# Self-attention over 2048 keys: the 32 steps as one written-out sequence instead of a loop of 8 steps on the engines

## The chip, the core and the metric

The kernel runs on one core of one Trainium2 chip. The metric is the device time of one execution in microseconds (us). The core has five engines that run their own instruction streams and meet only at semaphores: TensorE (PE; its weight loads are listed as PEld), VectorE (DVE), ScalarE (ACT), GpSimd (POOL) and SyncE (SP), which here issues the DMAs.

## The reference, cut to what matters

Two transformer blocks on x of shape 2 x 2048 x 512, with 16 heads of 32 channels: a cross-attention block, then a block of self-attention, cross-attention and MLP. The part around the change is the self-attention of the second block:

```python
def mha(q, k, v):                       # q, k, v: 2 x 2048 x 512, d = 32, H = 16
    scores = jnp.einsum('bqhd,bkhd->bhqk', qh, kh) / jnp.sqrt(d)
    attn = jax.nn.softmax(scores, axis=-1)
    out = jnp.einsum('bhqk,bkhd->bqhd', attn, vh)
    return out.reshape(B, Nq, C)
...
h = mha(q, k, v) @ self_o_w + self_o_b
x = x + h * gate_msa
```

## The kernel before, in words

`build` runs these stages one after the other: `conditioning`, `cross_pass` p1, `dense_pass` p2 (which makes q, k and v), `attention` a2 (from about 905 to 2807 us of the profiled span), `cross_pass` p3 and `mlp`. Only `attention` is touched.

`attention` works on 32 steps (`STEPS`). A step is one of 2 batches, one of 4 groups of 4 heads, and one of 4 chunks of 512 queries. Within a step PE makes the scores twice. In one form, queries on partitions (`score_unit`, tile a_sm, line L1797, 64 matmuls a step), DVE takes the maximum of each row (`peak_of_unit`, L1957), and from these `minus_peaks` (L1964 to L1973) makes the values that are subtracted. In the other form, keys on partitions (`score_tile`, tile a_st, L1819, 64 matmuls a step), ACT takes the exponential (`exponentials`, tile a_e, L1911). PE multiplies the exponentials with v (`weigh`, L1832) and adds them up (`add_up`, L1848) into tile a_acc; POOL adds part of them up beforehand (a_esum, L2029). Once a step ACT copies the two sums out (`fetch_sums`, tile a_sums, L1925), at the beginning of the step that follows; PE waits for this copy before it may write a_acc again. So the starts of the 32 a_sums copies cut the trace into steps: the copy of step n stands near the beginning of step n + 1. The peaks of a step are made two steps and one step ahead of its exponentials.

The order of the work on each engine is the order in which its function issues it; nothing reorders it. Each engine function ends in `run(engine, step, first, late)`. It writes out step 0 (for SP, steps 0 and 1), then opens a hardware loop, `engine.Fori(0, STEPS // BODY - 1)`, with `BODY` = 8 steps in its body, which is run 3 times, and then writes out what is left. On PE, steps 1 to 24 are in the loop and steps 25 to 31 are written out. In the loop the number of the iteration is in a register, so that every semaphore value that is waited for has to be worked out by register instructions (REGISTER_ALU in the listings below, ALU_OP and FUSED_REGOPS in the trace); in the written-out steps it is a constant. Each engine has its own loop and its own branch back (L1703), and the branches are not synchronized with each other.

`bank_of_unit` gives the PSUM bank of a score unit by `(j % BODY + u) % RING`. As 8 x 64 units aren't a multiple of the 3 banks, the sequence of banks breaks off at every eighth step, and `score_unit` then waits for one more read (`j % BODY == 0 and u < 2`).

Of the kernel before, what the change touches and what calls it, by code (L numbers as in the profile page):

```python
# [21 lines left out]
CHUNKS = T // W  # L22
# [1569 lines left out]
def attention(nc, d, name, q_in, k_in, v_in, o_out, keys, preload):  # L1592
# [21 lines left out]
    QR = 4  # L1614
# [2 lines left out]
    POOLED = [t for t in range(NKT - 2) if t % 3 != 2] if NKT > 2 else []  # L1617
    ADDS = max(len(POOLED) - 1, 0)
    STEPS = B * GROUPS * CHUNKS
    BODY = 2 * CHUNKS  # L1620
    TURN_KT = max(NKT - 3, 0)
    TURN = GH * (TURN_KT + 1)
    HEAD = 14 if NKT > 1 else U
# [5 lines left out]
    with nc.cleanup_on_exit(), ExitStack() as ctx:  # L1629
# [38 lines left out]
        def exists(i, j):  # L1668

            return not isinstance(i, int) or 0 <= BODY * i + j < STEPS  # L1670

# [4 lines left out]
        def number(i, j, p):  # L1676


            return (BODY * i + j) * TILES + p + (p < TURN or exists(i, j + 1))

        def turned(i, j):

            return number(i, j - 1, TURN) if j else 0
# [6 lines left out]
        def bank_of_unit(j, u):  # L1690

            return (j % BODY + u) % RING

# [4 lines left out]

        def run(engine, step, first, late):

            for j in range(first):
                step(0, j)
            with engine.Fori(0, STEPS // BODY - 1) as i:  # L1703
                for j in range(first, BODY + first):
                    step(i, j)
            for j in range(first, BODY + late):
                step(STEPS // BODY - 1, j)

        @block.sync
        def _(sp):  # L1710
            for dst, src in ((ident[:], d["ident"]), (mask[:], d["mask"])):
                sp.dma_start(dst, src).then_inc(small_in, DMA)
            for s in o_stored:
                sp.sem_inc(s, DMA)

            def load_q(i, j):

                for row, part in enumerate((0, 0, 1)):
                    src = q_in[part].rearrange("b (g h r) t -> (b g) r h t", g=GROUPS, h=GH)
                    sp.dma_start(q[row * DH:(row + 1) * DH, j % QR].bitcast(F32),  # L1720
                                 src[2 * i + j // CHUNKS, :, :, j % CHUNKS * W:(j % CHUNKS + 1) * W]
                                 ).then_inc(q_loaded[j % QR], DMA)

            def load_k(i, g):

                for row, part in enumerate((0, 1, 0)):
                    src = k_in[part].rearrange("b (g h r) t -> (b g) r h t", g=GROUPS, h=GH)
                    sp.dma_start(k[row * DH:(row + 1) * DH, g % 2, :, 0:keys].bitcast(F32),
                                 src[2 * i + g]).then_inc(k_loaded[g % 2], DMA)

            def load_v(i, g):
                sp.dma_start(v[0:KR, g % 2], v_in[(i + g // 2) // 2, :, bass.ds(((i + g // 2) % 2 * 2 + g % 2) * P, P)].rearrange("(t p) c -> p t c", p=KR)
                             ).then_inc(v_loaded[g % 2], DMA)

            def spread_rows(i, j):

                sp.wait_ge(score_read, turned(i, j) + 3)
                sp.dma_start(q[3 * DH:P, j % QR].bitcast(F32), rows[3 * DH:P, j % 2].unsqueeze(1).to_broadcast([DH, GH, W])
                             ).then_inc(rows_ready[j % QR], DMA)

            def store_o(i, j):
                sp.wait_ge(scaled, BODY * i + j + 3)


                sp.sem_inc(passed, 1)
                dst = o_out.rearrange("b (g p) t -> (b g) p t", p=P)
                sp.dma_start(dst[2 * i + j // CHUNKS, :, j % CHUNKS * W:(j % CHUNKS + 1) * W],
                             o[:, j % 2]).then_inc(o_stored[j % 2], DMA)

            def step(i, j):  # L1750
                if exists(i, j - 1) and exists(i, j + QR - 1):

                    sp.wait_ge(score_done, (BODY * i + j) * TILES + 1)
                    sp.sem_inc(passed, 1)
                if exists(i, j + QR - 1):
                    load_q(i, j + QR - 1)
                if j % CHUNKS == 0 and exists(i, j + CHUNKS):
                    load_k(i, j // CHUNKS + 1)
                    if exists(i, j - 1):

                        sp.wait_ge(tile_used, (BODY * i + j) * NKT + ER)
                        sp.sem_inc(passed, 1)
                    load_v(i, j // CHUNKS + 1)
                if exists(i, j - LATE - 1):
                    store_o(i, j - LATE - 1)
                if exists(i, j + 1):
                    spread_rows(i, j + 1)

                if isinstance(i, int) and i > 0 and 0 <= j - (BODY - QR) < len(preload):
                    sp.dma_start(*preload[j - (BODY - QR)]).then_inc(preloaded, DMA)  # L1770

            load_q(0, 0)
            load_k(0, 0)
            load_v(0, 0)
            for j in range(1, QR - 1):
                load_q(0, j)
            spread_rows(0, 0)
            run(sp, step, LATE + 1, LATE + 1)
            for s in o_stored:
                sp.wait_ge(s, DMA * (STEPS // 2 + 1))  # L1780
            sp.wait_ge(preloaded, DMA * len(preload))

        @block.tensor
        def _(pe):
# [103 lines left out]
            for u in range(HEAD):  # L1888
                score_unit(0, 1, u)
            run(pe, step, LATE, 1)  # L1890

        @block.scalar
        def _(act):
# [50 lines left out]
            act.activation(k[3 * DH:P, 0], mask[3 * DH:P].unsqueeze(2).to_broadcast([DH, GH, KC * KE]), ACT.Copy).then_inc(act_set_up, 1)  # L1944
            take_rows(0, 0)
            run(act, step, LATE, 1)

        @block.vector
# [286 lines left out]
def build(nc, d, out):  # L2235
# [17 lines left out]
    with nc.sbuf_tensor("mod", [P, MODS, B], F32) as mod:  # L2253
        def vector_of(tile):
            return lambda b, t: mod[:, tile + t, b:b + 1]

        with ExitStack() as ctx:
            raw_qkv, load_qkv = raw_weights(ctx, "raw_qkv", *[w("L1_xcond_qkv_w", c) for c in range(3)])
            with ExitStack() as inner:
                raw, load = raw_weights(inner, "raw_p1", d["L0_xcond_Wq"], d["L0_xcond_Wp"])  # L2260
                conditioning(nc, d, mod, gates, kv, load)
                cross_pass(nc, d, "p1", d["x"], x1, None, kv[0][0], kv[0][1], q, (1e-5, vector_of(0), vector_of(4)),
                           (1e-6, vector_of(20), vector_of(16)), d["L0_xcond_bq"], d["L0_xcond_bp"], u, raw, load_qkv)
            dense_pass(nc, d, "p2", u, [(vec("L1_xcond_qkv_b", 0), q), (vec("L1_xcond_qkv_b", 1), k)], (vec("L1_xcond_qkv_b", 2), v), raw_qkv)
        with ExitStack() as ctx:
            raw, load = raw_weights(ctx, "raw_p3", d["L1_xcond_self_o_w"], d["L1_xcond_q_w"], d["L1_xcond_cross_o_w"])
            attention(nc, d, "a2", q, k, v, o, T, load)
            cross_pass(nc, d, "p3", x1, x3, (o, d["L1_xcond_self_o_w"], d["L1_xcond_self_o_b"], gates[0]), kv[1][0], kv[1][1], q,
                       (1e-6, lambda b, t: mod[:, 40 + t, 0:1], lambda b, t: mod[:, 40 + t, 1:2]), (1e-6, vector_of(32), vector_of(28)),
                       d["L1_xcond_q_b"], d["L1_xcond_cross_o_b"], u, raw, [])  # L2270
        mlp(nc, d, u, x3, gates[1], out)
# [19 lines left out]
```

## Time and profile before

| what | value |
|---|---|
| device time, median of 3 runs | 4163.22 us (4161.48 to 4164.41) |
| device time of the profiled execution | 4159.49 us |
| span of the profiled execution, first to last instruction | 4157.7 us |
| mean granted TensorE clock | 0.938 of 2.4 GHz |
| PE busy | 3771.6 us, 91% |
| DVE / POOL / ACT busy | 2333.9 / 2080.2 / 1867.3 us, 56 / 50 / 45% |

The span runs from the first instruction to the last; 1.8 us of the profiled execution lie around it. A busy share is an average over stages that have different limits, so the rows below are cut to the attention stage. Of a timeline row the first number is the start, the second the duration, and in brackets stands how long the engine sat idle before it and what ended that. A matmul's duration overlaps the next one's; the pace of PE is read from the starts.

### The profile page before, as it was taken

Reading aid. Unit: us, or ns where it says so; the run is one execution under the profiler, and the core shown is the slowest. Engines: PE = TensorE matmul, PEld = TensorE weight load, DVE = VectorE, ACT = ScalarE, POOL = GpSimd, SP = SyncE. Lnnn points to the kernel's source line nnn. Section 1 sums busy time; section 2 is a strip of 40 time slices with the busy share of each in tenths; the row PEclk is TensorE's granted clock in tenths of the full one; section 3 lists DMA queues with packets and bytes.
Section 4 is the critical chain, followed back from the end, with each engine's and each line's share of the span. In section 5 each row is a group of like instructions: output and inputs, shape, how many; then the busy total and the mean of one; then the engine's idle time right before and its main releaser. Section 6 shows DMA issues by size and latency. Waiting matters only on the chain. (4 is left out here: it accounts for less than half of the span.)

```text
span 4157.7 us, 58861 instructions
## 1 busy us (share of the span) xinstructions
PE 3771.6 (91%) x19596; PEld 2442.6 (59%) x19596; DVE 2333.9 (56%) x4020; ACT 1867.3 (45%) x3431; POOL 2080.2 (50%) x923
## 2 busy tenths in 40 slices
PE   4799969979999999999999999985999959999998
PEld 2577748854444444444444444433777737888887
DVE  2466642247777767776777777733676625222222
ACT  1465631115666656665666666663565521111111
POOL 0356630005778767776777777783676634000000
PEclk8788879978999999999999999997999869999999
DMA  7566657752130211203130211105567651211110
GB/s 230 133 158 173 168 154 220 227 137 62 26 67 16 64 27 38 46 23 67 26 67 15 65 26 26 31 18 134 135 165 173 164 166 56 81 40 40 40 40 30
DMA packets 213560, 371.98 MB, mean 89 GB/s; under 512 B 36103, under 2 KB 52999, under 8 KB 209703
## 3 DMA queue, kind: packets, MB, share of 16 engines
q1 hardware_dynamic: 213287, 368.49, 32.7%
q8 instruction: 153, 2.51, 0.3%
q14 instruction: 120, 0.98, 0.1%
HBM read 215.54 MB, written 144.51 MB: 87 GB/s over the span
## 5 line engine op out<-in xcount | busy, mean ns | idle before, releaser
L1957 DVE TENSOR_REDUCE a_peak<-a_sm 128x1 f32<-128x512 f32 x2048 | 1275.0, 682 | 470.5 <-PE a_sm L1797 464.5
L1911 ACT ACTIVATE a_e<-a_st 128x512 f32<-128x512 f32 x2048 | 1075.1, 600 | 718.2 <-PE a_st L1819 714.7
L2029 POOL TENSOR_TENSOR a_esum<-a_esum,a_e 128x2048 f32<-128x2048 f32 x256 | 1172.1, 4578 | 126.5 <-ACT a_e L1911 114.1
L1819 PE MATMUL a_st<-a_q,a_k 128*128 128x512 f32 x2048 | 870.2, 428 | 17.9 <-issue 12.9
L1797 PE MATMUL a_sm<-a_k,a_q 96*128 96x512 f32 x2048 | 831.8, 413 | 49.7 <-DMA a_k<-s_k 28.1
L1819 PEld LDWEIGHTS a_st<-a_q,a_k 128*128 128x128 f32 x2048 | 386.4, 189 | 536.7 <-ACT a_e L1911 269.9
L1832 PE MATMUL a_acc<-a_e,a_v 128*32 128x512 f32 x4096 | 547.2, 606 | 17.6 <-ACT a_sums L1925 16.7
L1797 PEld LDWEIGHTS a_sm<-a_k,a_q 96*128 96x128 f32 x2048 | 397.8, 194 | 148.8 <-DVE a_peak L1957 57.6
L2152 PE MATMUL mlp_ph<-mlp_us,mlp_w_hi 128*128 128x512 f32 x1024 | 336.3, 391 | 31.9 <-DVE mlp_raw_lo L2201 31.9
L2029 POOL TENSOR_TENSOR a_esum<-a_e 128x2048 f32<-128x2048 f32 x32 | 146.8, 4587 | 427.6 <-ACT a_e L1911 427.6
L2194 ACT ACTIVATE mlp_gelu<-mlp_ph,mlp_b 128x512 f32<-128x512 f32 x128 | 88.1, 688 | 595.4 <-PE mlp_ph L2152 595.4
L2209 DVE CAST mlp_gs<-mlp_gelu 128x512 fp32r<-128x512 f32 x128 | 91.4, 714 | 458.3 <-ACT mlp_gelu L2194 458.3
L2167 PE MATMUL mlp_py<-mlp_w_hi,mlp_gs 128*128 128x512 f32 x1024 | 317.7, 391 | 17.1 <-DVE mlp_gs L2211 17.1
L2232 POOL TENSOR_TENSOR mlp_x<-mlp_x,mlp_brow 128x2048 f32<-128x2048 f32 x8 | 37.0, 4626 | 569.5 <-DMA mlp_x<-s_x 569.3
L1409 POOL TENSOR_TENSOR p_e<-p_e,p_inv 128x308 f32<-128x308 f32 x256 | 173.4, 709 | 168.6 <-DVE p_inv L1093 168.6
L2152 PEld LDWEIGHTS mlp_ph<-mlp_us,mlp_w_hi 128*128 128x128 f32 x1024 | 193.2, 189 | 72.6 <-issue 32.3
L2167 PEld LDWEIGHTS mlp_py<-mlp_w_hi,mlp_gs 128*128 128x128 f32 x1024 | 192.0, 188 | 61.6 <-issue 16.5
L587 PE MATMUL p_sm<-p_ks,p_qs 96*128 96x78 f32 x1024 | 171.9, 310 | 47.7 <-DMA p_qs<-s_q 28.3
L587 PEld LDWEIGHTS p_sm<-p_ks,p_qs 96*128 96x128 f32 x1024 | 157.2, 222 | 80.9 <-issue 28.9
L1848 PE MATMUL a_acc<-a_e,a_ones 128*32 128x512 f32 x1536 | 201.4, 596 | 1.7 <-POOL a_esum L2029 1.7
L2167 PE MATMUL mlp_py<-mlp_raw_lo,mlp_gs 128*128 128x512 f32 x512 | 200.0, 391 | 0.0
L2152 PE MATMUL mlp_ph<-mlp_us,mlp_raw_lo 128*128 128x512 f32 x512 | 199.9, 390 | 0.0
(151 smaller groups left out, 5169.7 us busy)
## 6 DMA issues: line engine op xcount, KB each, us to landing
p_qs<-s_q SPq DMA_DIRECT2D x192, 256.0 KB, 5.7
s_q<-p_qo SPq DMA_DIRECT2D x64, 512.0 KB, 7.4
a_q<-s_q SPq DMA_DIRECT2D x96, 256.0 KB, 5.2
a_k<-s_k SPq DMA_DIRECT2D x24, 1024.0 KB, 15.5
s_x<-p_x SPq DMA_DIRECT2D x16, 1024.0 KB, 4.4
s_u<-p_ut_hi SPq DMA_DIRECT2D x64, 256.0 KB, 5.8
s_u<-p_ut_lo SPq DMA_DIRECT2D x64, 256.0 KB, 6.4
p_us<-s_u SPq DMA_DIRECT2D x16, 1024.0 KB, 7.8
```

Source lines behind the costliest of these rows:

```text
L587: mm = pe.matmul(sm[:, unit % 2, h * KE:(h + 1) * KE], qs[0:3 * DH, g % 2, h, qt * P:(qt + 1) * P], ks[0:3 * DH, b, g * GH + h], start=Tru ...
L1409: pool.tensor_tensor(e[:, number % 2, qt, :, 0:S], e[:, number % 2, qt, :, 0:S], inv[:, number % 2, qt].unsqueeze(2).to_broadcast([P, GH, ...
L1797: mm = pe.matmul(sm[:, bank_of_unit(j, u), x * KE:(x + 1) * KE], q[0:3 * DH, j % QR, h, qt * P:(qt + 1) * P], k[0:3 * DH, g % 2, h, kc * K ...
L1819: pe.matmul(st[0:KR, place(kt, h) % RING], k[:, g % 2, h, kt * P:kt * P + KR], q[:, j % QR, h], start=True, stop=True).then_inc(score_done, 1)
L1832: mm = pe.matmul(acc[rows, 0], v[0:KR, g % 2, kt, rows], e[0:KR, (j * NKT + kt) % ER, h], start=(kt == 0), stop=(kt == NKT - 1), tile_posi ...
L1848: mm = pe.matmul(acc[h * DH:(h + 1) * DH, 1], ones[0:KR], operand[:, h], start=(kt == first), stop=(kt == NKT - 1 and x == len(operands) - ...
L1911: act.activation(e[0:KR, (j * NKT + kt) % ER, h], st[0:KR, place(kt, h) % RING], ACT.Exp, scale=SCALE).then_inc(score_read, 1)
L1957: dve.tensor_reduce(dst, src, AX.X, ALU.max).then_inc(unit_read, 1)
L2029: pool.tensor_tensor(esum[:], e[:, slot(0)] if x == 1 else esum[:], e[:, slot(x)], ALU.add).then_inc(e_added, 1)
L2152: mm = pe.matmul(ph[:, m % 4], w1[pw][:, t, m * P:(m + 1) * P], us[:, b, pm, t], start=(t == 0 and s == 0), stop=(t == KT - 1 and s == 2))
L2167: mm = pe.matmul(py[:, tt], gs[:, m % 2, pw, tt * P:(tt + 1) * P], w2[pm][:, m], start=(m == 0 and s == 0), stop=(m == HT - 1 and s == 2))
L2209: dve.tensor_copy(gs[:, m % 2, 0], gelu[:, m % 2]).then_inc(g_hi, 1)
```

## The change

`BODY` becomes 32, and `run` writes all steps out, on all five engines. The loop, its branches and the register instructions are gone, and every wait is against a constant. The condition under which SP preloads the weights of the next stage is adapted and holds at the same steps as before (28 to 30). With `j % BODY` now `j`, the banks go round without a break, and the additional read is asked for at step 0 alone, where it was already given.

```diff
-    BODY = 2 * CHUNKS
+    BODY = STEPS
...
         def run(engine, step, first, late):
 
-            for j in range(first):
+            for j in range(STEPS + late):
                 step(0, j)
-            with engine.Fori(0, STEPS // BODY - 1) as i:
-                for j in range(first, BODY + first):
-                    step(i, j)
-            for j in range(first, BODY + late):
-                step(STEPS // BODY - 1, j)
...
-                if isinstance(i, int) and i > 0 and 0 <= j - (BODY - QR) < len(preload):
+                if 0 <= j - (BODY - QR) < len(preload):
```

The lines below the edit move up by five: L1797 becomes L1792, L1819 becomes L1814, L1925 becomes L1920.

PE at the end of the loop's body, late in step 8 (and 16 and 24), before the change: L1688 and L1795 are the register instructions for a wait, L1703 is the loop's end.

```order
 L1848 MATMUL a_acc<-a_e,a_ones 32x512 x4
 L1819 MATMUL a_st<-a_q,a_k 128x512
 L1795 REGISTER_ALU
 L1797 MATMUL a_sm<-a_k,a_q 128x512
 L1688 REGISTER_ALU
 L1819 MATMUL a_st<-a_q,a_k 128x512
 L1795 REGISTER_ALU
 L1797 MATMUL a_sm<-a_k,a_q 128x512
 L1703 REGISTER_ALU
 L1703 COMPARE_AND_BRANCH
 L1819 MATMUL a_st<-a_q,a_k 128x512
```

The last of these rows is where the loop is left after step 24. The same place of a step after the change:

```order
 L1843 MATMUL a_acc<-a_e,a_ones 32x512 x4
 L1814 MATMUL a_st<-a_q,a_k 128x512
 L1792 MATMUL a_sm<-a_k,a_q 128x512
 L1814 MATMUL a_st<-a_q,a_k 128x512
 L1792 MATMUL a_sm<-a_k,a_q 128x512
 L1814 MATMUL a_st<-a_q,a_k 128x512
```

The matmuls stand in the same order; the register instructions and the branch between them are gone.

DVE where a step's peaks become the values to subtract, before the change (the last peak of a step, then L1962 to L1973, then the first peaks of the step after the next):

```order
 L1954 REGISTER_ALU
 L1957 TENSOR_REDUCE a_peak<-a_sm 128x1
 L1962 ISA
 L1964 TENSOR_REDUCE a_top<-a_peak 128x16
 L1966 TENSOR_SCALAR a_neg_hi<-a_top 128x16
 L1969 ISA
 L1972 COPY a_neg<-a_neg_hi 128x4x4
 L1973 SCALAR_TENSOR_TENSOR a_neg<-a_top,a_neg_hi 128x4x4
 L1953 REGISTER_ALU
 L1954 REGISTER_ALU
 L1957 TENSOR_REDUCE a_peak<-a_sm 128x1 x2
```

And after it:

```order
 L1952 TENSOR_REDUCE a_peak<-a_sm 128x1 x17
 L1959 TENSOR_REDUCE a_top<-a_peak 128x16
 L1961 TENSOR_SCALAR a_neg_hi<-a_top 128x16
 L1967 COPY a_neg<-a_neg_hi 128x4x4
 L1968 SCALAR_TENSOR_TENSOR a_neg<-a_top,a_neg_hi 128x4x4
 L1952 TENSOR_REDUCE a_peak<-a_sm 128x1 x21
```

Here too only the register instructions between the operations are gone.

## Rows read from the trace of the kernel before

**Rows 1.** The page: busy time of the engines in the whole span.
```profile
PE 3771.6 (91%) x19596; PEld 2442.6 (59%) x19596; DVE 2333.9 (56%) x4020; ACT 1867.3 (45%) x3431; POOL 2080.2 (50%) x923
```

**Rows 2.** All instructions on the tile a_sums: durations min/median/max, first and last start.
```profile
L1925 ACT ACTIVATE a_sums<-a_acc x32: 1024/1027/1032, 1015.3 to 2803.0; 128x1024 f32<-128x1024 f32 x32
```

**Rows 3.** Busy time in windows cut at starts of a_sums copies; columns in the first line.
```profile
core 0: us, PE busy (x) PEld busy (x) DVE busy (x) ACT busy (x) POOL busy (x), PEclk, DMA share, GB/s
1015.30:1417.19 401.89, 392.85 (x2213) 192.99 (x2212) 303.02 (x498) 247.14 (x470) 296.93 (x70) 1.00 0.15 34
1417.19:1483.81 66.62, 58.80 (x318) 28.46 (x316) 43.49 (x72) 35.40 (x69) 42.41 (x10) 0.92 0.40 90
1483.81:1885.72 401.91, 392.88 (x2213) 193.00 (x2212) 302.99 (x498) 247.02 (x470) 296.92 (x70) 1.00 0.15 34
1885.72:1951.88 66.16, 58.34 (x318) 28.36 (x316) 43.49 (x72) 35.41 (x69) 42.41 (x10) 0.95 0.41 91
1951.88:2411.34 459.46, 449.01 (x2529) 220.65 (x2528) 346.37 (x569) 282.30 (x537) 339.43 (x80) 1.00 0.19 42
2411.34:2697.50 286.16, 280.38 (x1581) 138.00 (x1580) 216.99 (x356) 178.31 (x336) 212.23 (x50) 1.00 0.10 27
```

**Rows 4.** PE's timeline over the end of the loop's first run.
```profile
1468.93 0.40 PE L1797 MATMUL a_sm<-a_k,a_q 96*128 96x512 f32 x1
1475.77 0.80 PE L1819 MATMUL a_st<-a_q,a_k 128*128 128x512 f32 x1 [6.44 <-issue]
...
1482.29 0.50 PE L1819 MATMUL a_st<-a_q,a_k 128*128 128x512 f32 x1
```

**Rows 5.** PE's timeline over the end of the loop's second run.
```profile
1944.28 0.80 PE L1819 MATMUL a_st<-a_q,a_k 128*128 128x512 f32 x1 [6.44 <-issue]
...
1950.36 0.50 PE L1819 MATMUL a_st<-a_q,a_k 128*128 128x512 f32 x1
```

**Rows 6.** PE's timeline where the loop is left, after its third run.
```profile
2405.53 0.40 PE L1797 MATMUL a_sm<-a_k,a_q 96*128 96x512 f32 x1
2406.00 0.47 PE L1819 MATMUL a_st<-a_q,a_k 128*128 128x512 f32 x1
...
2409.83 0.50 PE L1819 MATMUL a_st<-a_q,a_k 128*128 128x512 f32 x1
```

**Rows 7.** PE's timeline where the loop is entered.
```profile
1009.54 0.40 PE L1797 MATMUL a_sm<-a_k,a_q 96*128 96x512 f32 x1
1009.91 0.50 PE L1819 MATMUL a_st<-a_q,a_k 128*128 128x512 f32 x1
```

**Rows 8.** PE's branch at the end of the attention's loop: ns min/median/max, first and last.
```profile
L1703 PEldq COMPARE_BRANCH  x3: 82/3568/3758, 1467.0 to 2403.6; - x3
```

**Rows 9.** The same for PE's branch at the end of the MLP's loop.
```profile
L2172 PEldq COMPARE_BRANCH  x4: 76/222/240, 3612.6 to 4143.7; - x4
```

**Rows 10.** DMA queues from 1464 to 1484 us, at the first branch back.
```profile
q8 instruction: 3, 0.05, 1.0%
```

**Rows 11.** DMA queues from 2420 to 2650 us, in written-out steps.
```profile
q8 instruction: 10, 0.16, 0.3%
```

**Rows 12.** DMA queues from 3620 to 4150 us, in the MLP's loop: all lines.
```profile
q1 hardware_dynamic: 11616, 23.07, 12.0%
```

**Rows 13.** PE's timeline at the change of steps, in the loop (step 13).
```profile
1754.33 0.39 PE L1819 MATMUL a_st<-a_q,a_k 128*128 128x512 f32 x1
1755.48 0.50 PE L1797 MATMUL a_sm<-a_k,a_q 96*128 96x512 f32 x1 [0.76 <-DVE a_peak L1957]
```

**Rows 14.** The same place in a written-out step (step 26).
```profile
2509.30 0.39 PE L1819 MATMUL a_st<-a_q,a_k 128*128 128x512 f32 x1
2510.30 0.50 PE L1797 MATMUL a_sm<-a_k,a_q 96*128 96x512 f32 x1 [0.62 <-DVE a_peak L1957]
```

**Rows 15.** PE's groups over the five written-out steps, 2411.34 to 2697.50 us.
```profile
L1797 PE MATMUL a_sm<-a_k,a_q 96*128 96x512 f32 x321 | 127.5, 397 | 3.2 <-DVE a_peak L1957 3.2
L1832 PE MATMUL a_acc<-a_e,a_v 128*32 128x512 f32 x640 | 85.2, 605 | 2.2 <-ACT a_sums L1925 2.2
```

## The prediction

> **What bounds the kernel now.** I read the page first. PE is busy 91% of the span, every other engine at most 59% [rows 1]. That points to PE, but a share over the whole span can't price an edit of one stage, so I cut the attention stage at the starts of the a_sums copies, of which there is one a step [rows 2], into the windows of [rows 3]. Their columns show which engine sets the pace: in the 401.89 us of steps 1 to 7 PE is busy 392.85 us (98%), DVE 303.02, POOL 296.93 and ACT 247.14, and the granted clock is 1.00. So PE is the bound inside attention, and only what holds up PE counts. The other four engines get rid of their loops too; they have 14 us or more to spare in each step of 57.4 us.
>
> The same windows hold the answer to most of the question, because the kernel before runs the same step in both forms. Steps 1 to 24 go through the loop, 25 to 31 are written out. [Rows 3]: 7 looped steps take 401.89 us (57.41 each), the next window is one step and takes 66.62, then 401.91 for 7, 66.16 for one, 459.46 for 8 (57.43 each), and then 286.16 us for five written-out steps, which is 57.23 each. The two long windows are steps 8 and 16, where the first two runs of the loop end. Step 24 also ends a run of the loop, but there the branch isn't taken, and its window has no such excess.
>
> **The change part by part.**
>
> *The two branches back.* The 22 ordinary looped steps take (401.89 + 401.91 + 459.46) / 22 = 57.42 us. Steps 8 and 16 exceed this by 9.20 and 8.74, together 17.94 us. The timeline says what they consist of. Between the last matmul before the branch (start 1468.93) and the first behind it (1475.77) lie 6.84 us, with PE idle for 6.44 and "issue" as the reason: no semaphore was late, the engine had no instruction [rows 4]. In ordinary code the two starts would be some 0.23 us apart, as 1009.54 lies 0.37 from its successor even with the loop's entry between them [rows 7]; so 6.6 us are lost. Then PE runs slowly: the durations are 0.80 where 0.50 is usual, the window's clock is 0.92, and the piece of work up to the next a_st after the additions takes 6.52 us (1475.77 to 1482.29) [rows 4]. The same piece where the loop is left takes 3.83 (2406.00 to 2409.83) [rows 6], so 2.7 us go to PE standing at its lower clock level of 1.2 GHz after the pause. 6.6 + 2.7 = 9.3, against 9.20 measured. The second time it is 6.6 + (6.08 - 3.83) = 8.85, against 8.74 [rows 5]. Both parts go when the pause goes.
>
> Is the pause really the branch's? PE's branch record is 3568 and 3758 ns long on two occasions and 82 ns on the third, which falls through [rows 8]. Queue q8, which carries instructions, made 3 transfers in the 20 us around the first branch [rows 10], and 10 in 230 us of written-out steps, one per 23 us [rows 11]. So behind a taken branch PE's instructions are fetched anew. In the MLP's loop, whose body is much shorter, q8 isn't in the list of queues at all [rows 12], and the branch that is taken lasts 222 to 240 ns [rows 9]. What is dear is thus not a branch but a branch to code that has to be fetched. Without the loop, nothing jumps, and the fetch runs ahead as it does in the written-out steps.
>
> A rule of the Trainium skill speaks against this sum. "Advanced Engine Details and Errata", section Control Flow Timing, puts a compare-and-branch at about 108 ns. By that the loop's three branches on PE would be worth 0.3 us, and the pauses would belong to something that stays. The trace agrees for the branch that falls through (82 ns) and not for the two that are taken into unfetched code (3568 and 3758 ns) [rows 8]; the rows decide, and the rule's case is the second rival below.
>
> *The register instructions.* A written-out step takes 57.23 us, a looped one 57.42 [rows 3], 0.19 less. One place where it comes from is the change of steps, where PE waits for DVE's peak reductions: 0.76 us idle in the loop [rows 13], 0.62 written out [rows 14], because DVE works out two wait values between its small operations and its next peak. Over 24 steps this makes 24 x 0.19 = 4.5 us. All of it is on PE's path, since PE is the bound. Over the five written-out steps PE has just 3.2 us of idle time before that place and 2.2 us before a_acc, where ACT copies the sums [rows 15]; no other wait is behind these, so no new one takes their place: the written-out steps show what is late next, and it is the same two waits, shorter.
>
> *Entry and exit of the loop.* At the entry two starts are 0.37 us apart instead of 0.23 [rows 7], 0.14 us, before the first window. The exit (0.47 instead of 0.23 us) [rows 6] lies in the last looped window and is counted.
>
> *The banks and the additional read.* These cost nothing before: the first units of step 8, at which the banks break off, are scored in steps 6 and 7, which lie in the 401.89 us of seven even steps [rows 3]. I take them at nothing. *The preload and all the DMAs* are issued by SP in the same order, at the same steps. *The loads of k and v at every fourth step* are issued in steps 4 to 24, which are all looped; the five written-out windows hold none. The window of 8 steps has two of them and 57.433 us a step, those of 7 steps have one and 57.413 [rows 3]. So a step with loads takes up to 0.18 us more (0.02 divided by 2/8 - 1/7), from register work for its additional waits or from the loads themselves. In the second case 6 x 0.18 = 1.1 us of the gain would be missing. I take the first, since the bulk of the difference between the forms is of that kind, and keep the other for the range.
>
> *Sum.* 17.9 + 4.5 + 0.14 = 22.6 us (the short way: 1396.04 us for steps 1 to 24 minus 24 x 57.232 = 22.5, plus the entry). Against the profiled execution's own 4159.49 us this gives 4136.9. That execution was 3.7 us faster than the median of the runs shown, 4163.22; from the median I get 4140.6 us, and this is what I predict.
>
> *Bounds.* At the low end the steps keep their looped pace and only the branches go: 17.9, that is 4145.3. The high end: the largest excess that looped windows show, 57.43, against 57.23 for every step, and half a microsecond for entry and exit, is 17.9 + 4.8 + 0.5 = 23.2, that is 4140.0. To these comes what the runs differ by, 2.9 us from fastest to slowest. The stages behind attention shift by 22 us as a whole; their work is unchanged, and I put them at nothing, plus or minus the runs' own difference. The range is 4137 to 4147.
>
> **The rivals.**
>
> *Only the branches pay.* The step's pace could stay at 57.42, if the written-out steps at the end are faster for another reason, such as the missing loads of k and v. For it: the five steps are the last ones and hold fewer transfers (27 GB/s against 34) [rows 3]. Against it: a shorter idle time at a place that has to do with DVE and not with a load [rows 13, 14]. Time 4145.3.
>
> *The pause isn't the branch's.* The pauses stand at the end of steps 8 and 16, just behind the loads for a new group of heads and two steps behind the break of the banks; if something of this kind made PE wait, the pause would stay, and only the register instructions and the loop's ends would be gained: 4.5 + 0.14 = 4.6, time 4158.6. For it: only two events, at equal distance. Against it: PE's idle time is "issue" [rows 4, 5], the end of step 24 is the same place behind such loads and such a break, and has no pause [rows 6], and the branch's own record is long [rows 8].
>
> *Slower: fetching the long code isn't hidden.* The place is PE's instruction stream in steps 1 to 24, the price one exposed fetch per 23 us. There would be 24 x 57.2 / 23 = 60 of them. One takes about 0.3% of 16 x 230 us over 10, 1.1 us [rows 11]; exposed in full they cost 66 us, and the kernel would take 4163.2 + 66 - 22.6 = 4206.6. It decides from 22.6 / 60 = 0.38 us a fetch on. Against it: in the five written-out steps 12 fetches passed and PE's only idle times are the two waits for DVE and ACT [rows 15]. For it: just that what was seen of written-out attention code ran with few other transfers.
>
> *The change doesn't do what it says* is out: the listing has no branch between the steps.
>
> **How the numbers follow.** The forecast 0.73, only the branches 0.13, the pause stays 0.05, exposed fetches 0.05, something unnamed 0.04. What can be told from no change in a measurement of this kernel is about 0.2%, 8.3 us: below 4154.9 it is faster. The forecast, the first rival and half of the unnamed are faster: 0.88. The second rival and a little of the unnamed are within 0.2%: 0.06. The rest, 0.06, is slower. The range 4137 to 4147 holds the forecast and the first rival, 0.86 less a little for their tails.
>
> **What would show each step right or wrong.** In the profile of the changed kernel, with windows cut at the a_sums copies: steps 1 to 24 in about 1373.6 us, every step at 57.2 to 57.3, steps 8 and 16 like the others; no COMPARE_BRANCH in attention; the granted clock at 1.00 from step 1 to the end of attention without a dip at a step; q8 with one transfer per 23 us all the way; PE idle 0.62 us at the change of steps in all steps. The forecast is wrong if a pause with the reason "issue" stands anywhere in attention, if steps that load k and v are slower than the others by more than 0.2 us, or if the stages after attention change by more than 3 us.

## The result, and the profile after

| | before | after |
|---|---|---|
| median of 7 runs | 4163.22 us | 4144.30 us |
| lowest to highest | 4154.85 to 4166.21 | 4137.23 to 4152.43 |
| ratio of the runs | | 0.9957, 95% interval 0.9944 to 0.9969 |
| profiled execution, its span | 4159.49, 4157.7 | 4145.81, 4144.0 |

By the medians the kernel is faster by 18.9 us; the interval of the ratio gives 12.9 to 23.3. Predicted were 22.6 us and 4140.6, with a range of 4137 to 4147. The ratios in this text compare fast runs with fast runs; one execution of the kernel with PE alone written out, of 11039.88 us, is left out of them.

The page of the profile after has the same 19596 matmuls; the program as executed has 51860 records instead of 58861. Register and branch instructions are 7769 fewer, and 768 more instructions on semaphores stand in the written-out code.

```profile
span 4144.0 us, 51860 instructions
PE 3766.3 (91%) x19596; PEld 2441.2 (59%) x19596; DVE 2335.7 (56%) x4020; ACT 1877.2 (45%) x3431; POOL 2080.8 (50%) x923
```

The windows below are cut at the starts of the a_sums copies, as in [rows 3], with the same columns: steps 1 to 7, step 8, steps 9 to 15, step 16, steps 17 to 24, steps 25 to 29.

```profile
1011.13:1412.07 400.94, 392.72 (x2214) 193.22 (x2212) 303.94 (x498) 249.88 (x471) 297.10 (x70) 1.00 0.15 34
1412.07:1469.37 57.30, 56.12 (x318) 27.60 (x316) 43.43 (x72) 35.67 (x69) 42.45 (x10) 1.00 0.45 100
1469.37:1870.47 401.10, 392.80 (x2214) 193.23 (x2212) 303.98 (x498) 249.79 (x471) 297.15 (x70) 1.00 0.15 34
1870.47:1927.77 57.30, 56.12 (x318) 27.60 (x316) 43.43 (x72) 35.67 (x69) 42.45 (x10) 1.00 0.46 100
1927.77:2386.00 458.23, 448.87 (x2529) 220.84 (x2528) 347.34 (x569) 285.58 (x538) 339.57 (x80) 1.00 0.19 42
2386.00:2672.50 286.50, 280.57 (x1581) 138.02 (x1580) 217.13 (x356) 178.36 (x337) 212.25 (x50) 1.00 0.10 26
```

Steps 8 and 16 went from 66.62 and 66.16 us to 57.30 each, at a granted clock of 1.00. Steps 1 to 24 take 1374.87 us instead of 1396.04, 21.2 less. PE's timeline where the first pause stood [rows 4]:

```profile
1463.55 0.40 PE L1792 MATMUL a_sm<-a_k,a_q 96*128 96x512 f32 x1
1464.02 0.47 PE L1814 MATMUL a_st<-a_q,a_k 128*128 128x512 f32 x1
1464.34 0.40 PE L1792 MATMUL a_sm<-a_k,a_q 96*128 96x512 f32 x1
```

0.47 us from start to start instead of 6.84. The remainder over 0.23 us was there at the exit of the loop too [rows 6], and so was never the loop's. The same holds where the loop was entered [rows 7], here after the change:

```profile
1005.31 0.40 PE L1792 MATMUL a_sm<-a_k,a_q 96*128 96x512 f32 x1
1005.78 0.47 PE L1814 MATMUL a_st<-a_q,a_k 128*128 128x512 f32 x1
```

Here too the starts are 0.47 us apart, against 0.37 with the loop's entry between them. The queue q8 over steps 1 to 24:

```profile
q8 instruction: 59, 0.97, 0.3%
```

59 transfers of instructions in 1375 us, one per 23 us, as in [rows 11], and no idle time of PE with the reason "issue".

The stages around attention aren't touched, but they aren't equal. The two windows below are those behind the last a_sums copy up to the MLP's first matmul, of the trace before and of the trace after:

```profile
2802.97:3426.20 623.23, 492.35 (x2689) 388.22 (x2689) 334.52 (x663) 304.99 (x553) 360.88 (x323) 0.86 0.58 154
```

```profile
2777.99:3412.40 634.41, 500.86 (x2688) 395.48 (x2688) 333.50 (x663) 305.49 (x553) 360.64 (x323) 0.84 0.58 151
```

11.2 us more, at a lower mean clock. This stage took 615.7 to 627.7 us in the 13 other traces of this case, so the trace after stands alone with 634.4. In front of the first a_sums copy the second trace is 4.2 us faster (1011.13 against 1015.30). So 21.2, plus 4.2, minus 11.2, and minus 0.5 in steps 25 to 31 and the MLP, make up the 13.7 us between the two spans, and a whole-kernel difference of single traces says little here.

### The profile page after: what moved, and what is told of

It is laid out like the page before. It is cut to its first block and busy times, and to the rows that moved or that the text cites. A ratio compares the mean times of both kernels' runs of the same rounds, so it can differ in the third digit from the quotient of the medians.

```text
span 4144.0 us, 51860 instructions
## 1 busy us (share of the span) xinstructions
PE 3766.3 (91%) x19596; PEld 2441.2 (59%) x19596; DVE 2335.7 (56%) x4020; ACT 1877.2 (45%) x3431; POOL 2080.8 (50%) x923
## 5 line engine op out<-in xcount | busy, mean ns | idle before, releaser
L1814 PE MATMUL a_st<-a_q,a_k 128*128 128x512 f32 x2048 | 868.3, 427 | 6.7 <-ACT a_e L1906 4.5
L1792 PE MATMUL a_sm<-a_k,a_q 96*128 96x512 f32 x2048 | 831.0, 413 | 47.5 <-DMA a_k<-s_k 28.0
L1814 PEld LDWEIGHTS a_st<-a_q,a_k 128*128 128x128 f32 x2048 | 386.0, 189 | 523.8 <-ACT a_e L1906 256.6
L1792 PEld LDWEIGHTS a_sm<-a_k,a_q 96*128 96x128 f32 x2048 | 396.9, 194 | 145.9 <-DVE a_peak L1952 55.5
```

What stands on the lines that cost most here:

```text
L1792: mm = pe.matmul(sm[:, bank_of_unit(j, u), x * KE:(x + 1) * KE], q[0:3 * DH, j % QR, h, qt * P:(qt + 1) * P], k[0:3 * DH, g % 2, h, kc * K ...
L1814: pe.matmul(st[0:KR, place(kt, h) % RING], k[:, g % 2, h, kt * P:kt * P + KR], q[:, j % QR, h], start=True, stop=True).then_inc(score_done, 1)
```

## The experiments

The runs had to say where the gain comes from. The theory has two sources: PE's two instruction fetches behind its taken branches, and register work on DVE's way to PE. The rivals name other engines' branches, the banks, or register work alone. For each run the text gives its ordinary steps, its steps at the ends of the loop's runs, and steps 1 to 24 as a whole, all from its own trace, cut as above. The ratio is to runs of the kernel before on the same chip.

**The banks undone.** All steps written out, with `BODY` still 8 in the formulas:

```diff
-            with engine.Fori(0, STEPS // BODY - 1) as i:
+            for i in range(STEPS // BODY - 1):
```

> All 32 steps are written out on all engines, but the banks still break off at every eighth step and the additional read is still asked for (one part of the change undone). Theory (the gain is PE's two instruction fetches behind the taken branches, and the register work): no pause anywhere in attention, steps 1 to 24 in 1375 us as in the changed kernel, all within 0.5 us; ratio to before 0.995 to 0.996. Rival (the break of the banks or the additional read holds PE up and was part of the pause): 2 us or more of idle time near steps 6, 14 and 22, and steps 1 to 24 above 1380 us.

Steps between 57.23 and 57.27 us, a shorter and a longer one in turn; steps 1 to 24 in 1374.0 us; ratio 0.9952 (0.9936 to 0.9969). No pause. The banks and the additional read cost nothing, as predicted.

**PE written out, the others in their loops.** The same edit in PE's call of `run` alone.

> PE's steps are written out, the other four engines keep their loops. Theory: PE's own pause of 6.4 us is gone at both places. DVE still goes back: its branch at 1469.45 was followed by its next instruction at 1474.34, 4.9 us later, and PE may be only three score banks ahead of it, so 1 to 3 us of PE's time are lost behind each of the two branches, without a fall of the clock; steps 8 and 16 at 58.5 to 61 us, the other steps at 57.3 to 57.4. Rival 1 (the pause is not PE's own fetch, but comes from another engine): steps 8 and 16 stay at 66 us. Rival 2 (PE's fetch is all there is): they are at 57.4.

```profile
1417.25:1474.64 57.39, 55.54 (x314) 26.82 (x312) 41.61 (x69) 35.28 (x68) 42.40 (x10) 1.00 0.46 101
1474.64:1533.03 58.39, 57.05 (x320) 28.18 (x320) 45.01 (x75) 35.50 (x69) 42.43 (x10) 1.00 0.10 24
1934.71:1992.75 58.04, 57.10 (x319) 28.21 (x320) 44.65 (x75) 35.36 (x68) 42.39 (x10) 1.00 0.10 25
```

These are steps 8, 9 and 17. The pause is gone; the other engines' branches cost PE 1.0 and 0.7 us, at the beginning of the next step rather than in step 8, and less than I had allowed. Ordinary steps take 57.38, so nearly all of the register work that costs time isn't PE's. One small part is: of the steps that load k and v, 8 and 16 hold the pauses and 24 the loop's exit, and the other three, 4, 12 and 20, took 57.49 to 57.50 us in the kernel before where steps without loads took 57.40, and with PE written out they take 57.38 like the rest. The first line is step 4 before, the second step 4 with PE written out:

```profile
1187.49:1244.99 57.50, 56.12 (x317) 27.57 (x316) 43.29 (x72) 35.29 (x68) 42.41 (x10) 1.00 0.45 100
1187.71:1245.09 57.38, 56.10 (x317) 27.59 (x316) 43.34 (x72) 35.27 (x68) 42.40 (x10) 1.00 0.45 100
```

Ratio 0.9960 (0.9945 to 0.9975).

**PE alone in its loop.**

> The reverse: PE alone keeps its loop, the others' steps are written out. Theory: both pauses are as in the kernel before, 6.4 us idle and then a fall of the granted clock, steps 8 and 16 at 66 us; the other steps lie between 57.3 and 57.4. Rival (another engine's branch is behind it): no pause.

Steps 7, 8 and 16 and the timeline at the first branch:

```profile
1354.10:1411.32 57.22, 56.09 (x317) 27.57 (x316) 43.34 (x72) 35.64 (x69) 42.43 (x10) 1.00 0.10 20
1411.32:1478.89 67.57, 58.98 (x318) 28.45 (x316) 43.52 (x72) 35.74 (x68) 42.43 (x10) 0.92 0.39 88
1879.70:1947.07 67.37, 58.46 (x318) 28.38 (x316) 43.53 (x72) 35.73 (x68) 42.44 (x10) 0.92 0.41 89
```

```profile
1462.88 0.40 PE L1802 MATMUL a_sm<-a_k,a_q 96*128 96x512 f32 x1
1470.61 0.79 PE L1824 MATMUL a_st<-a_q,a_k 128*128 128x512 f32 x1 [7.33 <-issue]
```

Both pauses are there, and a little longer than before (10.3 and 10.1 us over an ordinary step). Ordinary steps are at 57.21 to 57.30 although PE does all its register work, except that steps 4, 12, 20 and 24 take 57.33 to 57.48. I had expected 57.3 to 57.4 for all. Ratio 0.9995 (0.9984 to 1.0007): with PE's loop alone nearly all of the gain is gone.

The queues say whose fetches these are. Over steps 1 to 24, first with PE alone in its loop, then with PE alone written out:

```profile
q8 instruction: 76, 1.25, 0.4%
q8 instruction: 60, 0.98, 0.3%
```

The kernel before has 76 on q8 too, the changed kernel 59: q8 goes with PE's loop. The other instruction queue, q14, goes with the other engines' loops (68 in the kernel before and with PE alone written out, 35 with PE alone in its loop and in the changed kernel).

**A loop of 16 steps, run once.**

> The loop stays, but its body is 16 steps and it is run once: steps 1 to 16 use register values for their waits, and no branch is ever taken back. At step 16 the banks meet so that the first unit waits for the last read of step 15 (up to 1 us once). Theory: no pause of 6.4 us; steps 1 to 16 at 57.40 but for entry and exit, steps 17 to 24 at 57.23 to 57.30; so steps 1 to 24 in 1376 to 1379 us, against 1396 with two branches taken and 1375 all written out. Rival (the register work is what costs, the branch is cheap): two thirds of the 21 us stay, 1389 us.

A loop that is run once turned out to be built with constants, without register work (51875 records, against 51860 all written out). So this run is one more written-out kernel and doesn't tell the two costs apart: steps 57.23 to 57.27, steps 1 to 24 in 1374.1 us, ratio 0.9957 (0.9942 to 0.9973).

**The changed kernel again.**

> The changed kernel once more, on the chip of the runs beside it, for a second trace of it: two questions are open. First, its steps 3 to 31 went at 57.30 us where three other kernels whose PE code is written out went at 57.25; if that is a matter of how the engines happen to stand to each other, it can come out at either value here; if it belongs to the program, it is 57.30 again. Second, in its first trace the stage behind attention (from PE's first matmul of p3 to its first of the MLP) took 598.7 us, against 586 to 588 in the five other traces; I expect 586 to 590 here, since its program is the same there. Ratio to before 0.995.

Steps 1 to 24 in 1373.9 us (57.25 each), 22.1 less than before. So 57.30 isn't a property of the program; what sets one pace or the other wasn't found. The stage behind attention took 627.7 us by the cut used above, between the 623.2 of before and the 634.4 of the first trace; up to PE's first matmul of p3 36 us of it pass, so by the expectation's cut it is 591.8, above what I expected. Ratio 0.9961 (0.9948 to 0.9973).

**A branch to near code.** On PE, behind steps 8 and 16 of the changed kernel:

```diff
+                if engine is near and j in (8, 16):
+                    with engine.Fori(0, 2) as again:
+                        engine.sem_inc(spare, 1)
```

> The changed kernel with a loop of two rounds on PE behind steps 8 and 16, whose body is one semaphore increment: two branches are taken, but back to an instruction just before them. Theory (what costs is fetching the instructions, not the branch): under 0.5 us of PE's time at each, no fall of the granted clock; steps 8 and 16 at 57.2 to 57.8. Rival (every branch taken on PE stops it for 6 us): steps 8 and 16 at 66 us.

```profile
L1705 PEldq COMPARE_BRANCH  x4: 76/145/222, 1466.6 to 1924.9; - x4
```

```profile
1416.82:1474.03 57.21, 56.09 (x318) 27.66 (x316) 43.36 (x72) 35.64 (x69) 42.38 (x10) 1.00 0.45 101
1874.68:1931.92 57.24, 56.09 (x317) 27.68 (x316) 43.42 (x72) 35.63 (x69) 42.41 (x10) 1.00 0.46 100
```

The branches are taken, last 0.22 us at most, and steps 8 and 16 are as short as the others. So a taken branch costs PE nothing that can be seen in a step; what costs is a branch back to code that isn't at hand. The traces show the fetch itself. In the kernel before, with PE alone in its loop and in the two further looped kernels below, a 16 KB transfer of q8 starts 1.0 to 1.5 us behind the start of PE's branch record, at all eight branches back, and the branch record (3.4 to 3.9 us) ends behind it; behind the two near branches that are taken none starts within 5 us. Between 1466 and 1472 us, at the first branch of the kernel before (from 1466.97):

```profile
q8 instruction: 1, 0.02, 1.2%
```

Ratio 0.9956 (0.9942 to 0.9970).

**DVE alone in its loop.**

> DVE alone keeps its loop, the other four engines are written out. With PE alone in the loop ordinary steps went at 57.24, with all but PE in it at 57.38. Theory (the register work that costs time is DVE's, between a_neg_hi and the next peak): ordinary steps at 57.35 to 57.40, PE idle 0.75 us at the change of steps; behind DVE's two branches PE loses 0.5 to 1 us, as with four engines in their loops. Rival (ACT's or POOL's register work): 57.25.

Ordinary steps took 57.40 to 57.48 us, even a little more than with four engines in their loops, and the steps behind the branches (9 and 17) 58.35 and 57.73. PE waits 0.82 us for DVE at the change of steps here (4.9 us over six changes), a little more than the 0.75 expected. So DVE's register work is enough for the whole difference between 57.25 and 57.40. Ratio 0.9971 (0.9961 to 0.9981).

**What PE waits for there.** The written-out kernel's DVE and POOL at the change of steps (starts and durations, of the trace after):

```profile
1737.20 0.22 DVE L1959 TENSOR_REDUCE a_top<-a_peak 128x16 f32<-128x64 f32 x1
1737.45 1.85 DVE L1961 TENSOR_SCALAR a_neg_hi<-a_top 128x16 fp32r<-128x16 f32 x1
1739.34 0.18 DVE L1967 COPY a_neg<-a_neg_hi 128x16 f32<-128x16 f32 x1
1739.42 0.18 DVE L1968 SCALAR_TENSOR_TENSOR a_neg<-a_top,a_neg_hi 128x16 f32<-128x16 f32 x1
```

```profile
1734.68 4.59 POOL L2024 TENSOR_TENSOR a_esum<-a_esum,a_e 128x2048 f32<-128x2048 f32 x1
1739.53 4.56 POOL L2024 TENSOR_TENSOR a_esum<-a_esum,a_e 128x2048 f32<-128x2048 f32 x1 [0.25 <-ACT a_e L1906]
```

An operation on 16 columns takes 1.85 us and ends at 1739.30, just behind POOL's add at 1739.27; the next two, at the gap between two adds, take 0.18. This is so in 31 of the 32 steps: whenever the operation starts, it ends 32 to 40 ns behind the end of the running add. If DVE is held by the add, PE's wait hangs on it. First I exchanged the two operations for another form:

```diff
-dve.tensor_scalar(neg_hi[:], top[:], -1.0, None, ALU.mult)
+dve.scalar_tensor_tensor(out=neg_hi[:], in0=top[:], scalar=-2.0, in1=top[:], op0=ALU.mult, op1=ALU.add)
```

> In every step DVE's a_neg_hi (128x16) takes 1.8 us and ends some 35 ns behind the POOL add that runs at that time. Here the written-out kernel makes a_neg_hi and the copy behind it with scalar_tensor_tensor, the form of the operation after them, which took 183 ns; values are the same. Theory (the DVE operation is held until POOL's add ends, and through it PE's wait at the change of steps): a_neg_hi under 0.4 us, PE's 0.62 to 0.67 us of idle time there gone, steps at 56.6 to 56.7 instead of 57.25 to 57.30, steps 1 to 24 in 1360 us, ratio to before 0.990 to 0.992. Rival 1 (the new form is held as well, or the operation is slow by itself): no change. Rival 2 (another wait takes its place): a_neg_hi short, step time within 0.1 us of 57.25.

```profile
L1961 DVE SCALAR_TENSOR_TENSOR a_neg_hi<-a_top x32: 176/1822/1856, 942.1 to 2711.7; 128x16 fp32r<-128x16 f32 x32
```

The theory failed here: 1.82 us in this form too, steps as before (1374.2 us for 24), ratio 0.9958 (0.9945 to 0.9970). The minimum of 176 ns, where no add ran, shows that the operation isn't slow by itself. The same in the kernel before:

> The same two operations exchanged in the kernel before, with its loop. Theory: the register work costs time only where PE waits for DVE at the change of steps, so without this wait the looped step is no slower than the written-out one, 56.6 to 56.8, with the two pauses of 9 us left as they are. Rival (the register instructions cost time elsewhere too): a looped step stays 0.13 us or more above that of the run beside it.

As the wait was still there, this run couldn't tell: steps 57.40, pauses of 9.3 us each, ratio 0.9996 (0.9986 to 1.0007). The one operation that ran beside an add and was never held is a_top's tensor_reduce. So all four became reductions:

```diff
-dve.tensor_reduce(top[:], src, AX.X, ALU.max)
-dve.tensor_scalar(neg_hi[:], top[:], -1.0, None, ALU.mult)
+dve.tensor_reduce(pair[:, :, 0].bitcast(F32), src, AX.X, ALU.max, negate=True)
+dve.tensor_reduce(pair[:, :, 1], src, AX.X, ALU.max)
...
+dve.tensor_reduce(parts[:, :, :, 0], by_head(pair)[:, :, :, 1:2], AX.X, ALU.max, negate=True)
+dve.tensor_reduce(parts[:, :, :, 1], by_head(pair), AX.X, ALU.add)
```

> The written-out kernel with the peaks' negation and splitting done by tensor_reduce alone (reductions over one or two elements, with negation), since in all traces a_top, a tensor_reduce of the same size at the same place, took 0.22 us beside a running POOL add while tensor_scalar (1.8 us) and scalar_tensor_tensor (1.8 us) ended with it. Values are the same. Theory (operations that need what POOL's two-input add holds are kept waiting, a reduction isn't): the chain from the last peak to the first peak of the next step takes about 1 us instead of 2.4, PE's 0.62 us of idle time at the change of steps is gone, steps at 56.6 to 56.7, attention some 18 us shorter than in the changed kernel. Rival (another wait takes over at once): chain short, steps at 57.1 or more.

DVE, POOL and the windows of steps 1 to 24:

```profile
1673.65 0.22 DVE L1960 TENSOR_REDUCE a_pair<-a_peak 128x16 f32<-128x64 f32 x1
1673.78 0.21 DVE L1961 TENSOR_REDUCE a_pair<-a_peak 128x16 fp32r<-128x64 f32 x1
1674.09 0.18 DVE L1967 TENSOR_REDUCE a_neg<-a_pair 128x16 f32<-128x16 f32 x1
1674.17 0.18 DVE L1968 TENSOR_REDUCE a_neg<-a_pair 128x16 f32<-128x32 f32 x1
```

```profile
1666.41 9.29 POOL L2023 TENSOR_TENSOR a_esum<-a_esum,a_e 128x2048 f32<-128x2048 f32 x2
```

```profile
1014.78:2368.08 1353.30, 1340.85 (x7586) 664.38 (x7585) 1000.85 (x1705) 855.53 (x1610) 1018.36 (x240) 1.00 0.19 43
```

The POOL row joins two adds; the four operations lie inside the second and take 0.7 us in all. Steps are at 56.39 us on average, 0.86 less than in the second trace of the changed kernel, and better than the 56.6 to 56.7 expected. PE's matmuls on a_sm over steps 1 to 24, second trace of the changed kernel and this one:

```profile
L1792 PE MATMUL a_sm<-a_k,a_q 96*128 96x512 f32 x1537 | 611.3, 398 | 14.7 <-DVE a_peak L1952 14.7
L1792 PE MATMUL a_sm<-a_k,a_q 96*128 96x512 f32 x1537 | 609.2, 396 | 0.0
```

Of the 20.6 us that the 24 steps lose, 14.7 are this wait. Some 5.7 more are busy time of PE (1346.5 us to 1340.9); why PE needs less of it no run shows. From the first to the last a_sums copy attention takes 1740.7 us against 1767.1, 26.4 less, where 18 were expected. Median 4113.29 us, ratio 0.9893 (0.9878 to 0.9908).

**The same with the loop.**

> The kernel before, with its loop, and the same tensor_reduce operations as in the run beside it. Theory (register work costs time only through PE's wait for DVE at the change of steps): if the run beside it loses that wait, ordinary looped steps here are within 0.05 us of its steps, and the two pauses stay at 9 to 10 us each. If the wait isn't lost there, this run tells nothing of it. Rival (it costs elsewhere too): 0.13 us or more apart.

```profile
1009.71:1404.37 394.66, 390.92 (x2213) 193.00 (x2212) 291.48 (x498) 247.10 (x470) 296.85 (x70) 1.00 0.16 34
1404.37:1469.29 64.92, 57.57 (x317) 28.23 (x316) 41.84 (x72) 35.40 (x69) 42.44 (x10) 0.95 0.41 93
1863.94:1930.21 66.27, 57.40 (x318) 28.23 (x316) 41.82 (x72) 35.39 (x69) 42.42 (x10) 0.95 0.42 91
```

Seven looped steps take 394.66 us, 56.38 each, no more than the 56.39 of the run beside it, as the theory says. Two small things speak against register work costing nothing at all: steps 4, 12 and 20 still take 56.47, and this kernel's own written-out steps 26 to 29 take 56.30, against 56.37 in its loop. So up to 0.07 us a step isn't excluded. The pauses remain, 8.5 and 9.9 us. Ratio 0.9934 (0.9919 to 0.9950).

**The MLP written out too.** In `mlp`, `Fori(0, CHUNKS)` became `for i in range(CHUNKS)` on all engines.

> The same as the written-out kernel with tensor_reduce, and the MLP's loop of four rounds written out as well, as the fastest version. In the MLP's loop a taken branch lasts 0.22 to 0.24 us on PE and no instruction fetch is made. Theory: writing it out gains 3 x 0.2 us at most, so the stage takes 730.5 to 731.6 us against 731.5; fetches appear and are hidden. Rival (its register work costs as much as attention's): several us less. Whole kernel 0.990 to 0.992 of before if the tensor_reduce theory holds.

The MLP's stage takes 731.8 us against 731.5 before: no gain where the loop's branch finds its target in place. The fetches appear as expected (24 on q8 in that stage against 6 in the kernel before) and are hidden. Median 4110.14 us, ratio 0.9899 (0.9886 to 0.9913), which can't be told from the run without it. These two are faster than both kernels of the case.

## Why the prediction was right, point by point

**The bound.** PE bounds attention, at 98% busy in both traces. Right; each microsecond that PE gained in steps 1 to 24 is in the stage.

**The two branches back, 17.9 us.** Right in size and cause. The windows of steps 8 and 16 lost 9.3 and 8.9 us, of which some 0.1 each belongs to the next term. PE in its loop alone keeps both pauses, PE alone written out has none, a branch to near code costs nothing, and the fetch stands in the traces behind each costly branch. One reading was off: at this place the two starts are 0.47 us apart without a branch too, not 0.23, so 6.4 us are lost in the pause and not 6.6, and with 2.7 at the lower clock it makes 9.1. The cost isn't a constant: over four kernels it was 8.5 to 10.3 us.

**The register instructions, 24 x 0.19 = 4.5 us.** The mechanism was right, the size somewhat too large: 57.42 went to 57.29 in the first trace and 57.25 in the second, 3.2 and 4.2 us. I took the five written-out steps at the end of the kernel before for the settled pace, 57.23. Five traces of kernels that are written out from the start lie at 57.23 to 57.26, and one at 57.29, 57.30 in most steps. I also gave only a part of it to DVE; the runs give nearly all of it to DVE (DVE alone in its loop 57.44, PE alone 57.24), and PE's share shows only at the steps with loads. It goes to 0.07 us or less in an ordinary step once PE doesn't wait for DVE.

**Loads of k and v, banks, preload.** At nothing, right: in the changed kernel steps with loads (4, 8, 12 ...) take 57.23 to 57.30 like the others, and the run with the old banks is no slower. In the loop steps 4, 12 and 20 took 0.10 us more, not up to 0.18, and it was PE's register work, the case that I took, since it is gone with PE alone written out.

**Entry and exit.** The 0.14 us were not there to gain: written out, the same two starts lie 0.47 us apart, more than with the loop's entry. The exit's 0.47 stayed too. I had compared a special place of the step with an ordinary one.

**The other stages, at nothing plus or minus 2.9 us.** This was too narrow, and my own sign for a wrong forecast, more than 3 us of change behind attention, came up with 11.2. By the same cuts the time outside attention in 14 traces lies between 2359.6 and 2377.1 us, whether or not PE has its loop (mean of the four traces with it, 2364; of the ten without it, 2368). The seven runs of the kernel before lie 11.4 us apart. Attention gained 20.2 to 22.0 us as a whole in the written-out kernels with the old DVE operations, and their medians 16.2 to 21.1. So the medians' gain came out below the 22.6 forecast every time, and that the time lies within 4137 to 4147 owes something to a range that is wider than these errors. Whether the missing 2 or 3 us are a real cost in the stages behind, or chance, wasn't settled.

**The rivals.** *Only the branches pay* falls with the steps at 57.25 to 57.30 in the middle of the stage, among the loads. *The pause isn't the branch's* falls with the two half-looped kernels. *Exposed fetches* falls too: there are 59 of them, and no "issue" pause in PE. The rule of the Trainium skill ("Advanced Engine Details and Errata", Control Flow Timing, about 108 ns) holds for the branch itself, 76 to 222 ns here, and says nothing of the fetch behind it.

## What to carry to other kernels

Look for a step that exists in both forms, in the loop and written out behind it: its windows price the change before it is made. Here a branch back cost PE 8.5 to 10.3 us where the loop's body had to be fetched again, and at most 0.24 us where it was short; a transfer on the instruction queue right behind the branch told the two cases apart. The register work that cost time lay on the way of a hand-over that PE waited for, so ask what that hand-over itself waits for: here it was worth more than the loop, 26.4 us of attention against 20.5.

## What the runs showed of the hardware

A DVE operation of 16 columns was held until POOL's running two-input add ended: 1.77 to 1.85 us as tensor_scalar (medians of the traces before and after), 1.82 as scalar_tensor_tensor, 0.18 where no add ran. A tensor_reduce of the same size took 0.18 to 0.22 us beside the add. The Trainium skill, "VectorE: DVE Perf Modes", section Two Vector instructions with no wait between them, has a second SBUF read interface that VectorE shares with GpSimd and that an operation uses if it has two SBUF tensors or runs in a two-port mode; the trace agrees, in that reductions, with one input, went through and scalar_tensor_tensor, with two, didn't. The tensor_scalar has one input as well; whether it ran in a two-port mode no row shows. Which of POOL's accesses holds it wasn't tried.

The pause behind PE's branch was 6.4 us of idle time in the kernel before, 7.3 and 7.7 with PE alone in its loop, 6.7 and 8.2 in the looped kernel with reductions, and each time followed by a stretch at 1.2 GHz (granted clock 0.92 to 0.95 in the step's window).
